# A gram product cut into two of 64 rows, and three accumulators on VectorE

## The reference

```python
def cin_layer(X0, Xi, W, b):                 # X0: (512, 39, 16), Xi: (512, Fi, 16)
    return einsum('hjk,bjd,bkd->bhd', W.reshape(H, 39, Fi), X0, Xi) + b[None, :, None]
e  = stack([tbl_f[ids[:, f]] for f in range(39)], axis=1)
x1 = cin_layer(e, e,  W0, b0)                # H = 128
x2 = cin_layer(e, x1, W1, b1)
x3 = cin_layer(e, x2, W2, b2)
z  = concatenate([x1.sum(2), x2.sum(2), x3.sum(2)], axis=1)
h  = relu(concatenate([z, dense_ctx], 1) @ W_top1 + b_top1)
y  = relu(h @ W_top2 + b_top2) @ W_top3
```

## Time and profile before

| | us |
|---|---|
| runs, median (lowest to highest of 3) | 657.04 (656.72 to 657.56) |
| span of the profiled execution | 664.5 |
| PE busy in that span | 633.7 (95%) |
| DVE, ACT, POOL busy | 561.9, 557.3, 443.1 |

### The profile page before, as it was taken

The page is one execution under the profiler, slowest core; times in us unless marked ns, Lnnn a source line. Parts: engine busy times, 40 slices in busy tenths (PEclk is TensorE's granted clock), DMA queues, the critical chain, the costliest instruction groups (busy, mean ns, idle before and its releaser), DMA issues.

```text
span 664.5 us, 11375 instructions
## 1 busy us (share of the span) xinstructions
PE 633.7 (95%) x2616; PEld 477.0 (72%) x2616; DVE 561.9 (85%) x878; ACT 557.3 (84%) x1940; POOL 443.1 (67%) x504
## 2 busy tenths in 40 slices
PE   2689999999999999999999999999999999989998
PEld 2656767777777777777777777777777777767874
DVE  3538788889899898989898989898989989899890
ACT  2348788989898999999998999998989998999773
POOL 7555897777777778687777787777777535152700
PEclk9799999999999999999999999999999999999999
DMA  8245533242424233242423333323242320200000
GB/s 292 22 61 105 162 38 87 51 87 56 84 56 80 59 58 84 40 102 33 90 41 84 57 86 55 87 52 81 57 85 55 67 68 6 69 27 0 1 0 1
DMA packets 91117, 43.58 MB, mean 66 GB/s; under 512 B 80630, under 2 KB 83780, under 8 KB 88943
## 3 DMA queue, kind: packets, MB, share of 16 engines
q1 hardware_dynamic: 84058, 41.77, 28.1%
q0 software_dynamic: 5120, 1.29, 2.2%
q10 hardware_dynamic: 1904, 0.15, 0.2%
HBM read 36.39 MB, written 1.81 MB: 57 GB/s over the span
## 4 chain that ended last, share of the span: by engine, by line
PE 75%; DVE 8%; ACT 7%; issue 6%; DMA 3%; DVEq 1%; POOL 0%; SPq 0%; another core or an unknown queue 0%
PE yb L1128 16%; PE yb L1124 16%; PE yb L1125 16%; PE p L1089 10%; PE pq L1101 6%; ACT yb L765 5%; DVE x L941 3%; DVE acc L935 3%; DMA gram<-in_L_rec_W_dram 2%; PE yb L1026 2%; DMA emb<-in_table_dram,idx 1%; DVE x1l L896 1%; PE yb L1237 1%; PE p L1182 1%; PE p L1214 1%
## 5 line engine op out<-in xcount | busy, mean ns | idle before, releaser
L765 ACT ACTIVATE yb<-yb,x0t 128x128 f32<-128x128 f32 x1728 | 467.2, 391 | 56.0 <-PE yb L1128 49.6
L935 DVE TENSOR_TENSOR acc<-acc,yb 128x512 f32<-128x512 f32 (+1 forms) x512 | 323.4, 674 | 33.8 <-ACT yb L765 30.9
L1124 PE MATMUL yb<-w1h,x1h 128*128 128x512 f32 (+1 forms) x640 | 293.8, 459 | 5.0 <-DVE acc L935 3.8
L1128 PE MATMUL yb<-w1h,x1l 128*128 128x512 f32 (+1 forms) x640 | 247.4, 387 | 0.0
L1125 PE MATMUL yb<-w1l,x1h 128*128 128x512 f32 (+1 forms) x640 | 247.1, 386 | 0.0
L497 POOL DMA_INDIRECT emb<-in_table_dram,idx x160 | 153.0, 956 | 53.1 <-issue 44.4
L1124 PEld LDWEIGHTS yb<-w1h,x1h 128*128 128x128 f32 x640 | 120.1, 188 | 59.4 <-DVE acc L935 25.3
L1125 PEld LDWEIGHTS yb<-w1l,x1h 128*128 128x128 f32 x640 | 120.5, 188 | 39.6 <-issue 18.0
L1128 PEld LDWEIGHTS yb<-w1h,x1l 128*128 128x128 f32 x640 | 120.1, 188 | 24.8 <-DVE x1l L896 0.4
L568 POOL TENSOR_TENSOR late<-late,x0r 117x512 f32<-117x512 f32 (+1 forms) x105 | 132.7, 1298 | 4.6 <-DMA late<-x_scratch 4.3
L544 POOL TENSOR_TENSOR bdiag<-mask,x0t 128x312 f32<-128x312 f32 x64 | 45.7, 714 | 107.0 <-PE pq L1101 106.4
(11 more groups left out here) (124 smaller groups left out, 377.2 us busy)
## 6 DMA issues: line engine op xcount, KB each, us to landing
late<-x_scratch SPq DMA_DIRECT2D x45, 312.0 KB
late<-x_scratch SPq DMA_DIRECT2D x30, 234.0 KB
x0r<-x_scratch SPq DMA_DIRECT2D x15, 234.0 KB
emb<-in_table_dram,idx POOLq DMA_INDIRECT x160
gram<-in_L_rec_W_dram SPq DMA_DIRECT2D x1, 2496.0 KB
late<-x_scratch SPq DMA_DIRECT2D x15, 156.0 KB
spare<-spare SPq DMA_DIRECT2D x28, 78.0 KB
x_scratch<-emb SPq DMA_DIRECT2D x75, 20.0 KB
```

Of the source, the lines that this page charges most:

```text
L765: op = act.activation(part, part, ACT.Copy, scale=x0t[u][:, t, j:j + 1])
L935: dve.tensor_tensor(part, part, parts(y_bank(t, m), n), ALU.add).then_inc(summed, 1)
L1124: pe.matmul(y[:, 0:w], hi, w1h[:, at:at + w], start=True, stop=False)
L1128: pe.matmul(y[:, 0:w], lo, w1h[:, at:at + w], start=False, stop=True).then_inc(bank_ready, 1)
```

## The change

A tile's gram becomes two products, rows 0 to 63 (samples 0 to 3) and rows 64 to 127 (samples 4 to 7), of 160 columns each, into two PSUM banks that lie side by side: the last 160 columns of DVE's second bank and the first 160 of pq. For this `bdiag` keeps four samples' columns, with a mask that repeats after 64 rows. The gram is issued behind bank 6 and copied behind bank 7. DVE's bank 6 gets an accumulator of its own, so that `acc` has 13 columns and DVE adds seven banks and not eight. Banks 0 and 6 now share one PSUM bank, and bank 3 shares its bank with the gram. The transposes of W2 move to other slots, and two start-up buffers move into the space of `gram`.

```diff
-N_ACC = 2
-BEGINS = DVE_BANKS[0:N_ACC]
+N_ACC = N_DVE
 PARTS = N_ACC * BANK_F + 1
 DVE_ORDER = (("sum before", 8), ("scale", 0), ("sum before", 9), ("scale", 3), ("sum", 1), ("sum", 2),
-             ("sum", 4), ("fold before", 0), ("scale", 6), ("sum", 5), ("sum", 7), ("sum", 6))
+             ("sum", 4), ("fold before", 0), ("scale", 6), ("sum", 5), ("sum", 7))
-SUM_ORDER = (1, 2, 4, 5, 7, 6, 8, 9)
+SUM_ORDER = (1, 2, 4, 5, 7, 8, 9)
+ACC_OF = {0: 0, 3: 1, 6: 2, 1: 0, 2: 1, 4: 0, 5: 2, 7: 1, 8: 0, 9: 2}
-GRAM_AT = 3
-GRAM_COPY_AT = 4
+GRAM_AT = 6
+GRAM_COPY_AT = 7
-W2_SLOTS = ((4, 6), (4, 9), (5, 6), (5, 9), (6, 9))
+W2_SLOTS = ((4, 2), (4, 9), (5, 2), (5, 9), (6, 2))
...
-        bdiag = [sb(f"bdiag{u}", [P, TILE_B, GRAM]) for u in range(2)]
+        bdiag = [sb(f"bdiag{u}", [P, HALF_B, GRAM]) for u in range(2)]
...
-        yb = [pb(f"yb{i}") for i in range(RING)]
+        two = pb("two", 2)
+        pq = two[:, 512:1024]
+        yb = [pb(f"yb{i}") for i in range(ACT_RING)] + [pb("yd0"), two[:, 0:512]]
+        gram_out = two[:, 512 - HALF_GRAM:512 + HALF_GRAM]
...
-            return yd[(t * N_DVE + DVE_BANKS.index(m)) % DVE_RING]
+            return yd[DVE_BANKS.index(m) % DVE_RING]
...
+            pool.tensor_tensor(mask[:, :], mask8[:, 0:HALF_B], mask8[:, HALF_B:TILE_B], ALU.add).then_inc(consts, 1)
...
-                pe.matmul(pq[:, 0:TILE_B * GRAM], x2[p][:, :], bdiag[p][:, :, :].rearrange("p b c -> p (b c)"),
-                          start=True, stop=True).then_inc(gram_done, 1)
+                pe.wait_ge(dve_scaled, (T + 2 if own is None else own) * N_DVE + 2)
+                for h in range(2):
+                    rows = slice(h * HALF_P, (h + 1) * HALF_P)
+                    op = pe.matmul(gram_out[:, h * HALF_GRAM:(h + 1) * HALF_GRAM], x2[p][rows, :],
+                                   bdiag[p][rows, :, :].rearrange("p b c -> p (b c)"), start=True, stop=True)
+                op.then_inc(gram_done, 1)
...
+                if m == DVE_BANKS[0]:
+                    if at_least(T, 1):
+                        bank_free(T - 1, DVE_BANKS[2])
+                elif m == DVE_BANKS[1]:
+                    if at_least(T, 3):
+                        pe.wait_ge(gram_copied, T - 2)
+                    elif at_least(T, 1):
+                        bank_free(T - 1, m)
+                elif m == DVE_BANKS[2]:
+                    bank_free(T, DVE_BANKS[0])
```

More of the change, by code:

```diff
@@ L45 @@
 GRAM = FIELDS + 1
+HALF_B = TILE_B // 2
+HALF_P = P // 2
+HALF_GRAM = HALF_B * GRAM
 ACT_BANKS = (1, 2, 4, 5, 7, 8, 9)
@@ L124, in sb, with pb @@
             return ctx.enter_context(nc.sbuf_tensor(name, shape, dt))
-        def pb(name):
-            return ctx.enter_context(nc.psum_tensor(name, [P, 512], F32))
+        def pb(name, banks=1):
+            return ctx.enter_context(nc.psum_tensor(name, [P, 512 * banks], F32))
         def sem(name):
@@ L133, in tower @@
         ident = sb("ident", [P, P])
-        mask = sb("mask", [P, TILE_B])
+        mask8 = sb("mask8", [P, TILE_B])
+        mask = sb("mask", [P, HALF_B])
         ids_all = sb("ids_all", [P, GROUPS, PER_Q], I32)
@@ L175, in tower @@
         w0sym = flat[:, 12288:12288 + CHUNKS * ROWS]
+        x0t3 = flat[:, 15360:15360 + TILES * ROWS].rearrange("p (t r) -> p t r", t=TILES)
+        x0a = flat[:, 15872:15872 + TILES * COLS].rearrange("p (t j) -> p t j", t=TILES)
         pairs = late[0:ROWS, :].rearrange("p (c n) -> p c n", c=CHUNKS)
@@ L461, in _ @@
             stack_weights()
-            sp.wait_ge(consts, 10)
+            sp.wait_ge(consts, 11)
             for at in CTX_AT:
@@ L501, in _ @@
             pool.memset(ident[:, :], 1.0).then_inc(consts, 1)
-            pool.memset(mask[:, :], 1.0).then_inc(consts, 1)
+            pool.memset(mask8[:, :], 1.0).then_inc(consts, 1)
             pool.wait_ge(consts, 1)
@@ L506, in _ @@
             pool.wait_ge(consts, 3)
-            pool.affine_select(out=mask[:, :], in_=mask[:, :], compare_op=ALU.is_ge, fill=0.0,
+            pool.affine_select(out=mask8[:, :], in_=mask8[:, :], compare_op=ALU.is_ge, fill=0.0,
                                base=0, pattern=[[-DIM, TILE_B]], channel_multiplier=1).then_inc(consts, 1)
             pool.wait_ge(consts, 4)
-            pool.affine_select(out=mask[:, :], in_=mask[:, :], compare_op=ALU.is_ge, fill=0.0,
+            pool.affine_select(out=mask8[:, :], in_=mask8[:, :], compare_op=ALU.is_ge, fill=0.0,
                                base=DIM - 1, pattern=[[DIM, TILE_B]], channel_multiplier=-1).then_inc(consts, 1)
             pool.wait_ge(consts, 5)
+            pool.tensor_tensor(mask[:, :], mask8[:, 0:HALF_B], mask8[:, HALF_B:TILE_B], ALU.add).then_inc(consts, 1)
+            pool.wait_ge(consts, 6)
             for u in range(2):
@@ L517, in _ @@
             pool.memset(dctx[:, :, :], 0.0).then_inc(consts, 1)
-            pool.wait_ge(consts, 9)
+            pool.wait_ge(consts, 10)
             pool.wait_ge(ids_in, 16 * 2)
@@ L544, in spread @@
                 pool.tensor_tensor(bdiag[t % 2][:, :, 0:FIELDS],
-                                   mask[:, :, None].to_broadcast([P, TILE_B, FIELDS]),
-                                   x0t[u][:, t, None, 0:FIELDS].to_broadcast([P, TILE_B, FIELDS]),
+                                   mask[:, :, None].to_broadcast([P, HALF_B, FIELDS]),
+                                   x0t[u][:, t, None, 0:FIELDS].to_broadcast([P, HALF_B, FIELDS]),
                                    ALU.mult).then_inc(bdiag_ready, 1)
@@ L737, in copy_gram @@
                 act.activation(gram[:, :, bass.ds(T * TILE_B, TILE_B)],
-                               pq[:, 0:TILE_B * GRAM].rearrange("p (b c) -> p c b", c=GRAM),
+                               gram_out.rearrange("p (b c) -> p c b", c=GRAM),
                                ACT.Copy).then_inc(gram_copied, 1)
@@ L908, in scale @@
                 dve.wait_ge(bank_ready, T * BANKS + m + 1)
[L909 to L919, removed]
+                if m == DVE_BANKS[0] and at_least(T, 2):
+                    dve.wait_ge(x2_ready, T - 1)
+                at = BANK_F * ACC_OF[m]
+                dve.tensor_tensor(acc[t % 2][:, :, at:at + BANK_F], parts(y_bank(t, m), BANK_F),
+                                  x0t[u][:, t, None, BANK_F * m:BANK_F * (m + 1)].to_broadcast([P, HID, BANK_F]),
                                   ALU.mult).then_inc(dve_scaled, 1)
@@ L923, in add_bank @@
                 n = fields_of(m)
-                k = SUM_ORDER.index(m)
-                if k < N_ACC:
-                    dve.wait_ge(dve_scaled, T * N_DVE + k + 1)
-                else:
[L928 to L933, removed]
+                earlier = [x for x in SUM_ORDER[0:SUM_ORDER.index(m)] if ACC_OF[x] == ACC_OF[m]]
+                if earlier:
+                    dve.wait_ge(summed, sums_by(T, earlier[-1]))
+                else:
+                    dve.wait_ge(dve_scaled, T * N_DVE + ACC_OF[m] + 1)
+                dve.wait_ge(act_scaled, T * N_ACT + ACT_BANKS.index(m) + 1)
+                at = BANK_F * ACC_OF[m]
                 part = acc[t % 2][:, :, at:at + n]
@@ L998, in _ @@
         def _(pe):
-            pe.wait_ge(consts, 9)
+            pe.wait_ge(consts, 10)
             pe.wait_ge(w0_sym, 2 * HALF + 1)
@@ L1094, in layer0, with gram_product @@
                     op.then_inc(l0_done, 1)
-            def gram_product(T, p):
+            def gram_product(T, p, own=None):
                 pe.wait_ge(x2_ready, T + 1)
@@ L1100, in gram_product @@
                     pe.wait_ge(gram_copied, T)
[L1101 to L1102 removed]
+                pe.wait_ge(dve_scaled, (T + 2 if own is None else own) * N_DVE + 2)
[4 more added lines that the diff above has]
+                op.then_inc(gram_done, 1)
             def bank_free(T, m):
[L1106 to L1107 removed]
+                if m in DVE_BANKS:
+                    pe.wait_ge(dve_scaled, T * N_DVE + DVE_BANKS.index(m) + 1)
                 else:
@@ L1112, in layer1_bank @@
                 T = g * TILES + t
[L1113 to L1118, removed]
+                if m == DVE_BANKS[0]:
[8 more added lines that the diff above has]
+                    bank_free(T, DVE_BANKS[0])
+                else:
+                    k = ACT_BANKS.index(m)
+                    if k >= ACT_RING:
+                        bank_free(T, ACT_BANKS[k - ACT_RING])
+                    elif at_least(T, 1):
+                        bank_free(T - 1, ACT_BANKS[k - ACT_RING])
                 y = y_bank(t, m)
@@ L1174, in _ @@
             period(GROUPS - 1, 1, 0)
-            gram_product(NT - 2, 0)
+            gram_product(NT - 2, 0, NT - 1)
             def layer2_plain(h):
@@ L1199, in _ @@
             first_terms(0)
-            gram_product(NT - 1, 1)
+            gram_product(NT - 1, 1, NT - 1)
             for c in range(1, TOP1 // P):
```

3 lines of the change are left out of this document (removed).

## The result

The changed kernel takes 668.03 us (median of 4 runs, 666.82 to 668.85) where the kernel before takes 657.30 on the same chip: ratio 1.0164, 95% interval 1.0149 to 1.0179. It is slower by 10.7 us; 646.9 was forecast.

What follows compares the result with a forecast made beforehand. PE was taken to bound the kernel, busy 95% of the span, with DVE and ACT 3 us behind in a group. A -6.0, B -7.6, C -1.0, D +3.8, E +0.7 sum to -10.1: 657.04 to 646.9, range 638 to 669.

Steps and rivals of the forecast that it cites:

- B: The gram on PE: its halves partly side by side, 0.40 not 0.54, change of rows at 0; -7.6 us.
- A: The seam on PE: the gram's 0.43 wait for the fold goes in 14 groups; -6.0 us.
- POOL "at nothing": POOL's wait for the later gram: net 2.6 later, covered by 3.0 of slack; without that cover, +4.
- fourth rival: TensorE empties between 64-row gram and 128-row bank: 683 at full restart, 669 at half; chance 0.22, most at 662 to 672.
- D: DVE: one sum less, longer fold, sum 5 right behind scale 6; +3.8 us, between 0 and +13.6.
- under 3 us of slack a group: DVE, part of D: a tile's net +0.08 lies under the 3 us DVE is behind PE in a group.
- third rival: DVE's chain takes the wait's place, scale 6 before bank 0: 656.7 us (653 to 658); chance 0.16.
- E: The last group's loop and the end: gram's 0.54 leaves, 0.56 and 0.12 enter; +0.7 us (-1 to +2).
- C: W2 transposes in group 1: PE's waits of 1.0 and 0.3 for ACT's copies; -1.0 us (0 to -1.3).
- the forecast's case: First rival, the sum of all parts: 646.9 us, 641 to 651 with D and A at their ends; chance 0.45.

Runs made afterwards that it cites:

- gram_twice: The changed kernel with every gram's two products issued twice, one pair behind the other: 683.68 us.
- moved_four_swap: moved_four with DVE's sum of bank 8 ahead of the fold at the seam: 657.44 us, ratio 1.0008 to the kernel before.
- moved_four_swap2: moved_four with DVE's sums of banks 8 and 9 both ahead of the fold at the seam: 653.29 us, ratio 0.9949 to the kernel before.
- full_rows: The changed kernel with both products of a gram on all 128 rows, bdiag keeping all eight samples: 668.46 us, ratio 1.0175 to the kernel before.
- one_product: The changed kernel with the gram as one product of 128 rows and 320 columns into pq: 668.39 us, ratio 1.0165 to the kernel before.
- after_four: The changed kernel with four buffers of bdiag, b1c in the space of gram: 667.40 us, ratio 1.0162 to the kernel before.
- three_only: The kernel before with three accumulators on DVE, changed PSUM use, gram as one product behind bank 3: 663.76 us, ratio 1.0107.
- after_four_128: after_four with both gram products on all 128 rows, one line different, the gram as such left out: 660.71 us, ratio 1.0064 to the kernel before.
- moved_four: The kernel before with gram and W2 transposes moved and four buffers of bdiag, not two: 658.88 us, ratio 1.0024.
- second trace of before: Trace of the kernel before with only two start-up buffers moved into the space of gram: 657.32 us, ratio 1.0006.

## Why the prediction was wrong

Two steps failed. The larger is B, which priced the change of rows at 0: it costs 0.40 a gram, and B came out at +7.3 in place of -7.6, 14.9 of the 21.1 us between 646.9 and 668.0. The other is A, "Nothing is left to wait for": 6.0 that were not there to gain.

A (-6.0): measured 0 in the changed kernel (0.57 lost at the seam before, 0.59 after), and +1.8 with the move by itself and POOL free. The rows showed it: sum 8 ends at 336.42 + 0.68 = 337.10, and bank 4, which waits for it, had its first product end at 337.16 + 0.51 = 337.67, 0.57 later; bank 1 ended 0.55 after its sum. The line of bank 4, from the kernel before:

```profile
337.16 0.51 PE L1124 MATMUL yb<-w1h,x1h 128*128 128x512 f32 x1
```

It stands 0.23 behind the gram's end too, so the two were level: bank 4 was on DVE's chain already, and the gram with its wait lay inside that time at no cost. Moved away, it left bank 4 waiting 0.59. The chain of waits in the changed kernel shows what that means: from tile 3's gram over bank 7 and ACT's scaling of it, then sum 7, fold and sum 8 to bank 4.

```profile
328.00 0.47 PE two L1104 x4
...
329.41 1.13 ACT yb L773 x4
...
332.96 0.69 DVE acc L934
333.69 0.50 PE yb L1138
```

Tile 0's gram, which stood beside DVE's part of this chain, now stands behind bank 4, so all four grams of a group lie on PE's part. The run gram_twice bears this out: its groups take 36.77, 1.07 more than the changed kernel's, and 4 x 0.27 is 1.08, so no wait hides any of the four. The question "what is late next" was answered for the fold alone, not for the sum behind it. moved_four_swap and moved_four_swap2 show the chain passing the wait from bank to bank until the fold is out of the way.

POOL "at nothing": the slack that I read, 3.0, is that of the first low part. The second one goes through SP's transfer to the slot behind bank 4 of tile 3. POOL's later start cost 8.0 us in the move alone. In the changed kernel this wait does not show, since the slower grams put PE later by about as much. SP's issue and PE's slot are 2.61 apart there, without a wait, and 2.64 in full_rows, with one; the changed kernel, then full_rows:

```profile
323.39 0.76 SPq L402 DMA_DIRECT2D spare<-spare  x1
326.00 0.39 PE L1075 MATMUL p<-spare,ctx_wide 117*128 117x512 f32 x1
...
322.81 0.76 SPq L402 DMA_DIRECT2D spare<-spare  x1
325.45 0.50 PE L1075 MATMUL p<-spare,ctx_wide 117*128 117x512 f32 x1 [0.35 <-DMA spare<-spare]
```

That is why neither undoing the split (full_rows, one_product) nor freeing POOL (after_four) gained anything alone. Both together gained 6.7.

B (-7.6): measured +7.3 by the gram's step, +6.7 by time. The overlap was better than forecast, 0.27 and not 0.40. The change of rows, priced at 0 from layer 0's 78 rows with no row of 64 to go by, costs 0.40 a gram, or 0.20 for each of its two changes on the mean, between the half restart (0.13) and the full one (0.26) of the fourth rival. That rival's case is the one that came true, at 668 in its 662 to 672, but its sum was right by luck: it held no full overlap, and A's gain. Two rules of the Trainium skill bear on this, and the runs agree with both. "TensorEngine Tiling (Array Packing)", section Key Properties, says that a change of the tiling mode drains TensorE. In these runs the change costs 0.40 there and back; the emptying itself stands in no row. "TensorE: Matmul & The Clock Gate", Part 3, has products on different groups of rows run at the same time. Here two halves take 0.27, as one does.

D (+3.8): the parts were nearly right (the fold 0.54 for 0.56, sum 5 0.21 for 0.12). What the accumulators cost, with the shared PSUM bank, depends on the rest: 7.0 us alone (three_only against 656.74), about 2 with the move and POOL free (after_four_128 is 4.1 above its before, moved_four 1.8). In that pair the groups are alike, 35.25 and 35.26, and the difference, 1.3 by the two traces, stands behind the last x1h. The "under 3 us of slack a group" did not hide it in three_only. The third rival's sign, waits for a scale before bank 0, stands in the changed kernel four times, 3.6 us in all, three of them in the last group.

E (+0.7): 1.6 behind the last x1h. C (-1.0) was not told apart; the 1.0 and 0.3 that it hoped for are of one trace, and the second trace of before has 0.3 and 0.3. Two lower ends of the prediction do not come out of their own terms, without bearing on the outcome: the 641 of the forecast's case is 639.7 by them, the 638 of the range 635.6. The 1.7 in the first two groups are from one trace each (after_four has 0.3), so start-up may differ by run; this stays open.

## What to carry to other kernels

Before a wait is counted as a gain, look at the next instruction on the waiting engine: if it starts just when the next link of the same chain ends, the wait is only passed on. An engine that waits for a moved instruction takes everything behind it along, through each queue down to the transfers. And when several limits lie within half a microsecond of each other, undoing one part shows nothing; free the neighbours first, then change the one thing.

## What the runs showed of the hardware

Two 64-row products into two PSUM banks ran wholly side by side: two passes each of 160 columns took 0.27 for both halves together, as for one. A change from 128 to 64 rows and back cost 0.40, with the granted clock at 1.00; how it splits between the two is not shown. Products of 78 rows between those of 128 showed no such cost.
